# Row sums of every other head group in the last walk of an attention kernel: from strips of ones on TensorE to adds on GpSimd

## The chip, the cores and the metric

The program runs on one core of one Trainium2 chip. The metric is device time in microseconds, from the start of the execution to its end; the time of a kernel is the median of its runs. All numbers are float32 (some matmul operands are the rounded float32 form of TensorE, with the remainder in a second operand).

## The reference

Three residual layers follow one another: cross attention of 128 rows of x on 2048 rows of context, a retention layer with a gated unit, and a layer of eight experts. The change lies in the first one. Cut to what matters:

```python
x = x + xattn(layernorm(x), ctx)          # x: 8 x 128 x 512, ctx: 8 x 2048 x 512

def xattn(query_states, key_value_states):
    q, k, v = ...                         # 16 heads of 32
    scores = einsum('bhtd,bhsd->bhts', q, k) + bias
    weights = softmax(scores, axis=-1)    # over the 2048 context rows
    attn = einsum('bhts,bhsd->bhtd', weights, v)
    return attn @ wo
```

The kernel divides by the sum of the exponents after it has mixed the values: for each batch, head and row t it needs the sum over all 2048 context rows of exp(score - shift). This sum is what the change computes on another engine.

## The kernel before, in words

`attention_phase` handles 8 batches (B). The context of a batch is cut into 4 chunks (C) of 512 rows, a chunk into 4 strips (ST) of 128 rows; the 16 heads lie in 4 groups (G) of 4 heads (HG). A unit u is one head group of one chunk: u = 16 * batch + 4 * chunk + group, 128 units in all (LAST_T). Each unit is walked twice. The first walk projects keys and values and finds the row maxima (`project`, `scores`, `maxima`). The second walk comes 16 steps later (LAG) and computes the turned scores, with context rows on the partitions (`scores_turned`, L584), adds bias and maximum to them (`shift_scores`, L468 and L469 on VectorE, result in `pT`), takes the exponents in place (`exponent`, L411 on ScalarE, two operations of two heads each) and mixes the values (`mix`, L602 on TensorE, into `o_bank`).

Every engine has its own hand-written loop over steps t, and its order is that of the program. In step t TensorE issues the turned scores of unit t - 16, then the projection and scores of the first walk, then the mix of unit t - 17. From step 129 on the first walk has run out, and only turned scores and mixes remain: this is the second walk of the last batch, u = 112 to 127 (u >= LAST_U), with the output of batch 6 between the mix of unit 114 and the turned scores of unit 116.

The sums of exponents are formed in two ways. For u < 112, `add_up` on GpSimd adds the four strips of `pT` into `total[:, g]` (L365 and L369, one 128 x 512 add each; the first chunk of a batch needs three, since the first add takes two strips). `sum_up` on TensorE then sums `total` over the partitions with a matrix of ones (L643), and `invert` on VectorE takes the reciprocal from bank `misc` (L499). For u >= 112, `mix` issues 16 more matmuls of ones with `pT` right behind its own (L612, "strips"; each float32 matmul shows as two in the trace, so 32 rows a unit), which accumulate in `kv_bank`, and one reciprocal at the end takes all four groups (L528). Then `divide` (L505), `output` (L664) and `residual` (L511) close the batch.

`pT` has two buffers, chosen by u % 2. `shift_scores(u)` therefore waits until unit u - 2 has been read: by its mix (`o_mm`) and, where GpSimd adds it, by its adds (`add_step`, counted by `adds_done`). The turned scores go through 5 ring banks (`RING_PLACE`), 4 of which a unit takes; TensorE waits for a bank until VectorE has shifted out of it (`shifted`). In a batch's first chunk the shift also needs `shift0`, which a DMA brings and GpSimd completes (`first_shift`, L353), in the order of its loop: `first_shift` ahead of `add_up` in a step. Each phase is a block of its own, and the next one begins when all engines have left it.

Of the kernel before, what the change touches and what calls it, by code (L numbers as in the profile page):

```python
# [72 lines left out]
    return RING_PLACE["s", HG * a + j]  # L73


def adds_done(u):

    return ST * (u + 1) - sum(1 for w in range(u + 1) if w // G % C == 0)


def query_phase(nc, env):
# [133 lines left out]
def attention_phase(nc, env):  # L215
# [5 lines left out]
    with ExitStack() as ctx:  # L221
# [43 lines left out]
        with nc.Block() as block:  # L265
# [75 lines left out]
            @block.gpsimd  # L341
            def _(pool):
                def low_part(n, i):
                    pool.wait_ge(ctx_hi_done, n * DC + i + 1)
                    pool.tensor_tensor(ctx_lo[:, n % 2, i, :], raw[:, i % 2],  # L345
                                       ctx_hi[:, n % 2, i, :].bitcast(F32), ALU.subtract).then_inc(ctx_lo_done, 1)

                def first_shift(i):

                    pool.wait_ge(shift0_in[i % 2], 16 * (i // 2 + 1))  # L350
                    pool.wait_ge(shift_out, i + 1)
                    for s in range(2):
                        pool.tensor_tensor(shift0[:, i % 2, :, s, :], shift0[:, i % 2, :, s, :], shift[:, i % G],  # L353
                                           ALU.add).then_inc(shift0_done, 1)

                def add_up(u):

                    m, g = divmod(u, G)
                    b, c = divmod(m, C)
                    pool.wait_ge(exp_done, 2 * (u + 1))  # L360
                    parts = [pT[:, u % 2, :, i, :] for i in range(ST)]
                    if c == 0:
                        if b:
                            pool.wait_ge(total_mm, (b - 1) * G + g + 1)
                        pool.tensor_tensor(total[:, g], parts[0], parts[1], ALU.add).then_inc(add_step, 1)  # L365
                        parts = parts[2:]
                    for i, part in enumerate(parts):
                        pool.wait_ge(add_step, adds_done(u) - len(parts) + i)
                        pool.tensor_tensor(total[:, g], total[:, g], part, ALU.add).then_inc(add_step, 1)  # L369

                pool.memset(ones[:], 1.0)
                for i in range(DC):
                    low_part(0, i)
                for t in range(STEPS):
                    n, g = divmod(t, G)
                    if n < B * C - 1:
                        low_part(n + 1, g)
                    i = t - SHIFT_STEP - 1
                    if i >= 0 and i % (C * G) < G and i // (C * G) < B:
                        first_shift(i // (C * G) * G + i % (C * G))  # L380
                    u = t - LAG
                    if 0 <= u < LAST_U:
                        add_up(u)

            @block.scalar
# [61 lines left out]
            @block.vector  # L447
            def _(dve):
                def shift_scores(u):

                    m, g = divmod(u, G)
                    b, c = divmod(m, C)
                    if u < 2:
                        dve.wait_ge(turned, 2 * G)
                    else:
                        dve.wait_ge(o_mm, u - 1)
                        if u - 2 < LAST_U:
                            dve.wait_ge(add_step, adds_done(u - 2))
                    if c == 0:
                        dve.wait_ge(shift_out, b * G + g + 1)  # L460
                        dve.wait_ge(shift0_done, 2 * (b * G + g + 1))
                    for j in range(HG):
                        sc = ring[ring_st(u, j)][:].rearrange("p (i t) -> p i t", i=ST)
                        dve.wait_ge(st_mm, HG * u + j + 1)
                        i0 = 0
                        if c == 0:
                            i0 = 2
                            dve.tensor_tensor(pT[:, u % 2, j, 0:2], sc[:, 0:2], shift0[:, g % 2, j], ALU.add)  # L468
                        dve.tensor_tensor(pT[:, u % 2, j, i0:], sc[:, i0:],  # L469
                                          shift[:, g, j].unsqueeze(1).broadcast_to([P, ST - i0, T]), ALU.add  # L470
                                          ).then_inc(shifted, 1)

                def maxima(a):

                    m, g = divmod(a, G)
                    b, c = divmod(m, C)
                    for j in range(HG):
                        h = HG * g + j
                        sc = ring[ring_s(a, j)]
                        dve.wait_ge(s_mm, HG * a + j + 1)  # L480
                        if c == 0:
                            i = b * G + g
                            if j == 0:
                                dve.wait_ge(bias_in[i % 2], 16 * (i // 2 + 1))
                            dve.tensor_tensor(sc[:, 0:BW], sc[:, 0:BW], bias[:, i % 2, j, :], ALU.add
                                              ).then_inc(biased, 1)
                            dve.wait_ge(biased, HG * i + j + 1)
                        dve.tensor_reduce(negm[:, c, h:h + 1], sc[:], AX.X, ALU.max, negate=True).then_inc(max_done, 1)  # L488
                    if c == C - 1:
                        hs = slice(HG * g, HG * g + HG)  # L490
                        dve.wait_ge(max_done, HG * (a + 1))
                        dve.tensor_reduce(mneg[:, hs], negm[:, :, hs].rearrange("p c h -> p h c"), AX.X, ALU.min
                                          ).then_inc(row_max, 1)

                def invert(i):
                    dve.wait_ge(total_mm, i + 1)
                    if i % G == 0 and i >= G:
                        dve.wait_ge(wo_mm, i // G)
                    dve.reciprocal(aT[:, i % G, :], misc[:, i % G * T:(i % G + 1) * T]).then_inc(rinv_done, 1)  # L499

                def divide(b):

                    dve.wait_ge(o_mm, (b + 1) * C * G)
                    dve.wait_ge(rinv_done, (b + 1) * G)
                    dve.tensor_tensor(aT[:], o_bank[:].rearrange("p (g t) -> p g t", g=G), aT[:], ALU.mult  # L505
                                      ).then_inc(o_done, 1)

                def residual(b):
                    dve.wait_ge(wo_mm, b + 1)
                    dve.wait_ge(x_in, 16 * (b + 1))  # L510
                    dve.tensor_tensor(x_row[:], misc[:], x_row[:], ALU.add).then_inc(x_done, 1)  # L511

                for t in range(STEPS):
                    if 0 <= t - LAG < LAST_T:
                        shift_scores(t - LAG)
                    if 1 <= t <= LAST_T:
                        maxima(t - 1)
                    i = t - TOTAL_STEP
                    if i >= 0 and i % (C * G) < G and i // (C * G) < B - 1:
                        invert(i // (C * G) * G + i % (C * G))  # L520
                        if i % (C * G) == G - 1:
                            divide(i // (C * G))
                    i = t - WO_STEP - 1
                    if i >= 0 and i % (C * G) == 0 and i // (C * G) < B - 1:
                        residual(i // (C * G))
                dve.wait_ge(o_mm, B * C * G)
                dve.wait_ge(wo_mm, B - 1)
                dve.reciprocal(aT[:], kv_bank[:].rearrange("p (g t) -> p g t", g=G)).then_inc(rinv_done, G)  # L528
                divide(B - 1)
                residual(B - 1)  # L530

            @block.tensor
            def _(pe):
# [56 lines left out]
                def mix(u):  # L590
# [8 lines left out]
                    for i in range(ST):  # L599
                        for j in range(HG):  # L600
# [2 lines left out]
                                           v[:, m % (C + 1), i, h * DH:(h + 1) * DH], pT[:, u % 2, j, i, :],  # L603
                                           start=(c == 0 and g == 0 and i == 0),
                                           stop=(c == C - 1 and g == G - 1 and i == ST - 1))
                    if u >= LAST_U:

                        if u == LAST_U:
                            pe.wait_ge(kv_out, 2 * LAST_T)
                        for i in range(ST):  # L610
                            for j in range(HG):
                                mm = pe.matmul(kv_bank[j * DH:(j + 1) * DH, g * T:(g + 1) * T], ones[:],  # L612
                                               pT[:, u % 2, j, i, :], start=(c == 0 and g == 0 and i == 0),
                                               stop=(c == C - 1 and g == G - 1 and i == ST - 1))
                    mm.then_inc(o_mm, 1)

# [50 lines left out]
                for t in range(STEPS):  # L667
# [18 lines left out]
                    i = t - WO_STEP  # L686
                    if i >= 0 and i % (C * G) == 0 and i // (C * G) < B - 1:
                        output(i // (C * G))
                output(B - 1)


# [1103 lines left out]
```

## Time and profile before

| | us |
|---|---|
| runs | 2053.71, 2054.47, 2055.05 |
| median | 2054.47 |
| profiled execution | 2055.39 |
| its span, first to last instruction | 2053.6 |
| TensorE busy in the span | 1886.2 (92%) |
| VectorE | 1130.7 (55%) |
| GpSimd | 804.0 (39%) |
| ScalarE | 777.9 (38%) |

The span leaves out 1.8 us before the first and after the last instruction of the profiled execution. A busy share is an average over phases with different limits. The second walk of the last batch lies between about 1243 us, where VectorE begins to shift unit 112, and 1307 us, where the last mix is done; the retention layer starts at about 1321 us. In the views below, PE is TensorE's matmuls, PEld its weight loads, DVE VectorE, ACT ScalarE and POOL GpSimd. A line of a timeline gives start and duration, in us, of several like instructions in a row (x4: four of them), and in brackets the idle time ahead of the first and what ended it.

### The profile page before, as it was taken

Reading aid. Unit: us, or ns where it says so; the run is one execution under the profiler, and the core shown is the slowest. Engines: PE = TensorE matmul, PEld = TensorE weight load, DVE = VectorE, ACT = ScalarE, POOL = GpSimd, SP = SyncE. Lnnn points to the kernel's source line nnn. Section 1 sums busy time; section 2 is a strip of 40 time slices with the busy share of each in tenths; the row PEclk is TensorE's granted clock in tenths of the full one; section 3 lists DMA queues with packets and bytes.
Section 4 is the critical chain, followed back from the end, with each engine's and each line's share of the span. In section 5 each row is a group of like instructions: output and inputs, shape, how many; then the busy total and the mean of one; then the engine's idle time right before and its main releaser. Section 6 shows DMA issues by size and latency. Waiting matters only on the chain. (4 is left out here: it accounts for less than half of the span.)

```text
span 2053.6 us, 40698 instructions
## 1 busy us (share of the span) xinstructions
PE 1886.2 (92%) x17102; PEld 1431.3 (70%) x17102; DVE 1130.7 (55%) x2160; ACT 777.9 (38%) x1295; POOL 804.0 (39%) x641
## 2 busy tenths in 40 slices
PE   7599999999999999999999999579879998599995
PEld 3477777677677677677677777367657877499995
DVE  4244656656656556657556557464765233455553
ACT  1233434344344434344344334241244130355552
POOL 0114677668668677667667662000000000100001
PEclk9899999999999999999999999789989997699998
DMA  8622121121121122122122101210041004799993
GB/s 166 209 88 87 53 73 56 54 79 58 48 78 58 52 73 63 47 76 70 38 78 68 35 30 33 90 52 14 1 139 31 1 1 173 281 368 358 359 359 110
DMA packets 101126, 210.82 MB, mean 103 GB/s; under 512 B 9088, under 2 KB 33968, under 8 KB 95840
## 3 DMA queue, kind: packets, MB, share of 16 engines
q1 hardware_dynamic: 99488, 204.02, 29.4%
q0 software_dynamic: 1472, 4.40, 0.7%
q8 instruction: 127, 2.08, 0.4%
q14 instruction: 39, 0.32, 0.1%
HBM read 187.68 MB, written 20.71 MB: 101 GB/s over the span
## 5 line engine op out<-in xcount | busy, mean ns | idle before, releaser
L369 POOL TENSOR_TENSOR total<-total,probT 128x512 f32<-128x512 f32 x392 | 502.7, 1282 | 231.6 <-ACT probT L411 207.5
L488 DVE TENSOR_REDUCE negm<-bank 128x1 f32<-128x512 f32 x512 | 326.8, 685 | 179.4 <-PE bank L572 175.0
L469 DVE TENSOR_TENSOR probT<-bank,shift 128x512 f32<-128x512 f32 (+1 forms) x512 | 291.2, 615 | 216.2 <-PE bank L584 216.2
L411 ACT ACTIVATE probT<-probT 128x1024 f32<-128x1024 f32 x256 | 271.2, 1060 | 227.4 <-DVE probT L469 214.6
L405 ACT ACTIVATE v<-bank 128x512 f32<-128x512 f32 x128 | 76.4, 597 | 478.3 <-PE bank L552 478.3
L345 POOL TENSOR_TENSOR ctx_lo<-ctx_raw,ctx_hi 128x512 fp32r<-128x512 f32 x128 | 165.7, 1295 | 153.2 <-ACT ctx_hi L391 148.9
L552 PE MATMUL bank<-ctx_hi,wkv_hi 128*128 128x512 f32 x512 | 152.1, 419 | 22.5 <-ACT ctx_hi L391 22.5
L602 PEld LDWEIGHTS bank<-probT,v 128*32 128x32 f32 x4096 | 104.0, 109 | 94.0 <-ACT probT L411 92.0
L584 PEld LDWEIGHTS bank<-q,k 32*128 32x128 f32 x4096 | 126.0, 186 | 46.5 <-issue 44.1
L1348 POOL MEMSET zero_sb<- 128x512 f32 x1 | 0.5, 525 | 393.2 <-POOLq L1118 393.2
L552 PE MATMUL bank<-wkv_hi,ctx_hi 128*128 128x512 f32 x512 | 152.6, 420 | 0.0
L584 PE MATMUL bank<-q,k 32*128 32x128 f32 x4096 | 150.2, 283 | 0.6 <-DVE probT L469 0.5
L572 PE MATMUL bank<-k,q 32*128 32x512 f32 x1024 | 147.7, 640 | 0.0
L1670 PEld LDWEIGHTS bank<-xslotT,w_sb 128*128 128x128 f32 x1280 | 146.0, 194 | 1.9 <-DVE xslotT L1617 1.2
L1670 PE MATMUL bank<-xslotT,w_sb 128*128 128x128 f32 x1280 | 146.3, 277 | 0.8 <-DVE xslotT L1617 0.8
L602 PE MATMUL bank<-probT,v 128*32 128x128 f32 x4096 | 138.4, 276 | 6.0 <-ACT probT L411 5.8
L552 PE MATMUL bank<-wkv_lo,ctx_hi 128*128 128x512 f32 x512 | 138.0, 391 | 0.0
L552 PE MATMUL bank<-ctx_hi,wkv_lo 128*128 128x512 f32 x512 | 137.8, 391 | 0.0
L552 PE MATMUL bank<-wkv_hi,ctx_lo 128*128 128x512 f32 x512 | 136.9, 389 | 0.0
L552 PE MATMUL bank<-ctx_lo,wkv_hi 128*128 128x512 f32 x512 | 136.8, 389 | 0.0
L1593 ACT ACTIVATE w_hi<-w_sb 128x512 fp32r<-128x512 f32 x160 | 87.1, 615 | 124.8 <-PE bank L1683 79.3
L552 PEld LDWEIGHTS bank<-ctx_hi,wkv_hi 128*128 128x128 f32 x512 | 87.8, 189 | 49.7 <-ACT ctx_hi L391 23.4
(236 smaller groups left out, 2800.8 us busy)
## 6 DMA issues: line engine op xcount, KB each, us to landing
w_sb<-w SPq DMA_DIRECT2D x10, 4096.0 KB, 14.2
w_sb<-w SPq DMA_DIRECT2D x40, 1024.0 KB, 6.3
ctx_raw<-ctxT SPq DMA_DIRECT2D x128, 256.0 KB, 3.2
bias<-bias_scratch SPq DMA_DIRECT2D x32, 512.0 KB, 5.3
shift<-turned_bias SPq DMA_DIRECT2D x32, 512.0 KB, 5.1
slots<-zero_sb SPq DMA_DIRECT2D x17, 256.0 KB, 3.0
bias_scratch<-btab SPq DMA_DIRECT2D x1, 3072.0 KB, 34.2
down_w<-down SPq DMA_DIRECT2D x11, 256.0 KB, 2.6
```

The costliest lines, as they stand in the source:

```text
L345: pool.tensor_tensor(ctx_lo[:, n % 2, i, :], raw[:, i % 2], ctx_hi[:, n % 2, i, :].bitcast(F32), ALU.subtract).then_inc(ctx_lo_done, 1)
L369: pool.tensor_tensor(total[:, g], total[:, g], part, ALU.add).then_inc(add_step, 1)
L405: act.activation(v[:, n % (C + 1), g, :], (o_bank if t < LAG else kv_bank)[:], ACT.Copy).then_inc(kv_out, 1)
L411: act.activation(pT[:, u % 2, j:j + 2], pT[:, u % 2, j:j + 2], ACT.Exp).then_inc(exp_done, 1)
L469: dve.tensor_tensor(pT[:, u % 2, j, i0:], sc[:, i0:], shift[:, g, j].unsqueeze(1).broadcast_to([P, ST - i0, T]), ALU.add).then_inc(shifted, 1)
L488: dve.tensor_reduce(negm[:, c, h:h + 1], sc[:], AX.X, ALU.max, negate=True).then_inc(max_done, 1)
L552: mm = pe.matmul(dst[:], lhs, rhs, start=(c == 0 and i == 0), stop=(c == DC - 1 and i == 2))
L572: pe.matmul(ring[ring_s(a, j)][:], q[rows, b % 3, g, :], k[rows, m % C, g, :], start=True, stop=True).then_inc(s_mm, 1)
L584: mm = pe.matmul(ring[ring_st(u, j)][:, i * T:(i + 1) * T], k[rows, m % C, g, i * P:(i + 1) * P], q[rows, b % 3, g, :], start=True, stop=True)
L602: mm = pe.matmul(o_bank[j * DH:(j + 1) * DH, g * T:(g + 1) * T], v[:, m % (C + 1), i, h * DH:(h + 1) * DH], pT[:, u % 2, j, i, :], start=( ...
L1593: cp = act.activation(w2_hi[:, j, :], w2[:, j, :], ACT.Copy)
L1670: mm = pe.matmul(bank[1 + j // 4][:, j % 4 * P:(j % 4 + 1) * P], w1[:, s, c, j * P:(j + 1) * P], xT[:, c, :], start=(c == 0), stop=(c == D ...
```

## The change

In the last batch, units with an even u (groups 0 and 2) are summed by `add_up` on GpSimd as in the other batches; units with an odd u keep their strips of ones. `shift_scores(u)` waits for `add_step` wherever GpSimd adds unit u - 2. At the end TensorE sums `total` of groups 0 and 2 over the partitions into `misc`, and VectorE takes four reciprocals of 128 columns, two from `misc` and two from `kv_bank`.

```diff
--- before.py
+++ after.py
@@ -73,9 +73,14 @@
     return RING_PLACE["s", HG * a + j]
 
 
+def added_on_pool(u):
+
+    return u < LAST_U or u % 2 == 0
+
+
 def adds_done(u):
 
-    return ST * (u + 1) - sum(1 for w in range(u + 1) if w // G % C == 0)
+    return sum(ST - 1 if w // G % C == 0 else ST for w in range(u + 1) if added_on_pool(w))
 
 
 def query_phase(nc, env):
@@ -379,7 +384,7 @@
                     if i >= 0 and i % (C * G) < G and i // (C * G) < B:
                         first_shift(i // (C * G) * G + i % (C * G))
                     u = t - LAG
-                    if 0 <= u < LAST_U:
+                    if 0 <= u < LAST_T and added_on_pool(u):
                         add_up(u)
 
             @block.scalar
@@ -454,7 +459,7 @@
                         dve.wait_ge(turned, 2 * G)
                     else:
                         dve.wait_ge(o_mm, u - 1)
-                        if u - 2 < LAST_U:
+                        if added_on_pool(u - 2):
                             dve.wait_ge(add_step, adds_done(u - 2))
                     if c == 0:
                         dve.wait_ge(shift_out, b * G + g + 1)
@@ -524,8 +529,11 @@
                     if i >= 0 and i % (C * G) == 0 and i // (C * G) < B - 1:
                         residual(i // (C * G))
                 dve.wait_ge(o_mm, B * C * G)
+                dve.wait_ge(total_mm, (B - 1) * G + 1)
                 dve.wait_ge(wo_mm, B - 1)
-                dve.reciprocal(aT[:], kv_bank[:].rearrange("p (g t) -> p g t", g=G)).then_inc(rinv_done, G)
+                for g in range(G):
+                    rc = dve.reciprocal(aT[:, g, :], (kv_bank if g % 2 else misc)[:, g * T:(g + 1) * T])
+                rc.then_inc(rinv_done, G)
                 divide(B - 1)
                 residual(B - 1)
 
@@ -603,14 +611,14 @@
                                            v[:, m % (C + 1), i, h * DH:(h + 1) * DH], pT[:, u % 2, j, i, :],
                                            start=(c == 0 and g == 0 and i == 0),
                                            stop=(c == C - 1 and g == G - 1 and i == ST - 1))
-                    if u >= LAST_U:
-
-                        if u == LAST_U:
+                    if not added_on_pool(u):
+
+                        if u == LAST_U + 1:
                             pe.wait_ge(kv_out, 2 * LAST_T)
                         for i in range(ST):
                             for j in range(HG):
                                 mm = pe.matmul(kv_bank[j * DH:(j + 1) * DH, g * T:(g + 1) * T], ones[:],
-                                               pT[:, u % 2, j, i, :], start=(c == 0 and g == 0 and i == 0),
+                                               pT[:, u % 2, j, i, :], start=(c == 0 and g == 1 and i == 0),
                                                stop=(c == C - 1 and g == G - 1 and i == ST - 1))
                     mm.then_inc(o_mm, 1)
 
@@ -686,6 +694,13 @@
                     i = t - WO_STEP
                     if i >= 0 and i % (C * G) == 0 and i // (C * G) < B - 1:
                         output(i // (C * G))
+                pe.wait_ge(shift_out, B * G)
+                for g in range(0, G, 2):
+                    pe.wait_ge(add_step, adds_done(LAST_T - G + g))
+                    for j in range(HG):
+                        mm = pe.matmul(misc[j * DH:(j + 1) * DH, g * T:(g + 1) * T], ones[:], total[:, g, j, :],
+                                       start=True, stop=True)
+                mm.then_inc(total_mm, 1)
                 output(B - 1)
 
 
```

## Rows read from the trace of the kernel before

**Rows 1.** Page, part 2: GpSimd's busy tenths in 40 slices of 51.3 us

```profile
POOL 0114677668668677667667662000000000100001
```

**Rows 2.** Timeline, all engines (start us, us, engine, line, operation, out<-in), units 117 to 119

```profile
1267.08 2.48 DVE L469 TENSOR_TENSOR probT<-bank,shift 128x512 f32<-128x512 f32 x4 [0.18 <-PE bank L584]
...
1268.41 2.25 ACT L411 ACTIVATE probT<-probT 128x1024 f32<-128x1024 f32 x2 [1.01 <-DVE probT L469]
...
1270.59 2.48 DVE L469 TENSOR_TENSOR probT<-bank,shift 128x512 f32<-128x512 f32 x4 [1.02 <-PE bank L584]
...
1270.71 1.08 PE L602 MATMUL bank<-probT,v 128*32 128x128 f32 x32 [0.21 <-ACT probT L411]
...
1271.61 1.06 PE L612 MATMUL bank<-probT,att_ones 128*32 128x128 f32 x32
...
1272.62 1.17 PE L584 MATMUL bank<-q,k 32*128 32x128 f32 x32
1273.86 2.48 DVE L469 TENSOR_TENSOR probT<-bank,shift 128x512 f32<-128x512 f32 x4 [0.78 <-PE bank L584]
```

**Rows 3.** Timeline of VectorE alone: shifts of units 116, 126 and 127, the last reciprocal

```profile
1263.82 2.48 DVE L469 TENSOR_TENSOR probT<-bank,shift 128x512 f32<-128x512 f32 x4 [2.58 <-PE bank L584]
...
1298.03 2.48 DVE L469 TENSOR_TENSOR probT<-bank,shift 128x512 f32<-128x512 f32 x4 [1.02 <-PE bank L584]
1301.29 2.48 DVE L469 TENSOR_TENSOR probT<-bank,shift 128x512 f32<-128x512 f32 x4 [0.78 <-PE bank L584]
1307.00 3.36 DVE L528 RECIPROCAL aT<-bank 128x512 f32<-128x512 f32 x1 [3.22 <-issue]
```

**Rows 4.** Windows: length, busy us (count) of PE, PEld, DVE, ACT, POOL; PEclk; DMA

```profile
1263.82:1298.03 34.21, 30.64 (x960) 26.67 (x952) 25.43 (x42) 21.08 (x20) 0.00 (x0) 1.00 0.06 19
```

**Rows 5.** GpSimd: timeline, and line L369's durations (min/median/max ns)

```profile
1123.74 1.28 POOL L365 TENSOR_TENSOR total<-probT 128x512 f32<-128x512 f32 x1 [2.60 <-ACT probT L411]
1125.09 2.66 POOL L369 TENSOR_TENSOR total<-total,probT 128x512 f32<-128x512 f32 x2
...
1248.79 2.51 POOL L353 TENSOR_TENSOR shift<-shift 128x512 f32<-128x512 f32 x2 [4.29 <-DMA shift<-turned_bias]
1255.80 2.50 POOL L353 TENSOR_TENSOR shift<-shift 128x512 f32<-128x512 f32 x2 [4.50 <-DMA shift<-turned_bias]
...
L369 POOL TENSOR_TENSOR total<-total,probT x392: 1263/1286/1297, 193.9 to 1240.8; 128x512 f32<-128x512 f32 x196
```

**Rows 6.** Timeline, all engines, 1234 to 1259 us: units 110 to 115, output of batch 6

```profile
1234.36 2.25 ACT L411 ACTIVATE probT<-probT 128x1024 f32<-128x1024 f32 x2 [1.91 <-DVE probT L469]
...
1236.69 5.37 POOL L369 TENSOR_TENSOR total<-total,probT 128x512 f32<-128x512 f32 x4 [1.89 <-ACT probT L411]
...
1245.54 1.06 ACT L411 ACTIVATE probT<-probT 128x1024 f32<-128x1024 f32 x1 [0.27 <-DVE probT L469]
...
1247.22 0.43 PE L643 MATMUL bank<-total,att_ones 128*32 128x128 f32 x8 [0.20 <-ACT shift L426]
...
1248.03 0.95 DVE L499 RECIPROCAL aT<-bank 128x128 f32<-128x128 f32 x1
...
1253.16 0.42 DVE L468 TENSOR_TENSOR probT<-bank,shift 128x256 f32<-128x256 f32 x1 [0.74 <-PE bank L584]
...
1257.94 1.06 PE L612 MATMUL bank<-probT,att_ones 128*32 128x128 f32 x32
1258.50 0.42 DVE L468 TENSOR_TENSOR probT<-bank,shift 128x256 f32<-128x256 f32 x1 [2.60 <-POOL shift L353]
...
1258.93 3.27 PE L664 MATMUL bank<-wo_sb,aT 128*128 128x512 f32 x7
```

**Rows 7.** Timeline of TensorE's matmuls in later phases, at the lower clock

```profile
1430.29 2.09 PE L1041 MATMUL bank<-qT,kT 32*128 32x128 f32 x32
...
1508.69 1.97 PE L1242 MATMUL bank<-ident,z 128*128 128x128 f32 x8 [2.89 <-DVE z L1186]
```

**Rows 8.** Window of TensorE: length, busy us (matmuls), mean granted clock, DMA share, GB/s

```profile
1507.00:1508.00 1.00, 0.00 (x0) 0.89 0.00 0
```

## Prediction

> **What bounds the kernel now.** The page's slices come first: GpSimd's digits are zero in the slices behind 1283 us [rows 1], although TensorE still works at attention there. So the engine that the change uses is free in that stage; what has to be found is what paces the stage. The chain of waits doesn't reach back this far, so I read the timeline of all engines over the last sixteen units, u = 112 to 127.
>
> One unit goes through the engines in this order: VectorE shifts its scores (four L469 operations), ScalarE takes exponents (two L411), TensorE mixes (L602), then the strips of ones (L612), then the turned scores of a later unit (L584). Follow unit 117 in [rows 2]: the shift starts at 1267.08; ScalarE runs from 1268.41 to 1270.66, 3.58 behind that start; the mix starts at 1270.71, the strips at 1271.61, the turned scores of unit 119 at 1272.62, and its shift at 1273.86. That loop is 6.78 us for two units. A second loop ties neighbours together: the five ring banks let the turned scores of a unit start only when three of the four shift operations of the unit before have read theirs. From the shift of 118 at 1270.59 to the turned scores of 119 at 1272.62 it is 2.03, and 1.24 more to the shift at 1273.86, so 3.27 for one unit. Two of those are 6.54, less than 6.78. **The pace of the stage is therefore the two-unit loop, strips included.** From the shift of 116 to that of 126 it is 34.21 us [rows 3], five pairs of 6.77 with one excess of 0.36.
>
> There are two interleaved copies of the two-unit loop: even units follow even units, odd units follow odd ones, and neither can run ahead of the other by more than the ring lets it. TensorE is busy 30.64 of these 34.21 us at the full granted clock [rows 4], but its mix waits for ScalarE in every unit, so it is not the work on TensorE alone that sets the pace.
>
> **The change, part by part.** *Removed:* the strips of the eight even units, 32 matmuls each, 1.06 us a group [rows 2]. This shortens only the even copy of the loop. The odd copy keeps its strips and its 6.78, and an even unit can't be followed by the next odd one any faster than that copy allows. In units 116 to 126 the removal alone is worth nothing. It is worth something in one place: between unit 114 and unit 116 the output matmuls of the batch before stand behind the strips of 114 on TensorE. The strips start at 1257.94 and the output at 1258.93, and the shift of 116 at 1263.82 waits for what follows that output [rows 3, 6]: 0.99 earlier.
>
> *Added on GpSimd:* the sums of eight units: three adds each for 112 and 114 (the first chunk begins with the sum of two parts), four each for 116 to 126. They start 0.08 behind the exponents: ScalarE ends at 1236.61, GpSimd starts at 1236.69, and the four take 5.37 [rows 6]. Three take 4.01, from 1123.74 to 1127.75 [rows 5]. The 392 adds of this line lie between 1263 and 1297 ns, beside any mix of VectorE and ScalarE work [rows 5], so I take the same durations here.
>
> *Added on VectorE:* the wait at the head of each shift. The kernel holds the exponents in two buffers by parity, so unit u overwrites what unit u-2 left. Before, this stage waited only for the mix of u-2; now an even unit also waits for GpSimd's sum of u-2. Queued behind that wait are this unit's shift, then the next odd unit's, and with them all exponents, mixes and turned scores: nothing in the stage runs past it.
>
> Price of the new loop, even unit to even unit: 3.58 from the shift to the end of the exponents [rows 2], 0.08 to GpSimd, 5.37 for four adds [rows 6], and the handover from GpSimd to VectorE. The only row that shows one is L353, which ends at 1258.30, and the shift behind it at 1258.50 [rows 5, 6]: 0.20. Together **9.23 us for two units, where 6.78 stood**. The odd unit between them follows at 3.27 and is hidden. From 116 to 126 this is five times 9.23, 46.15 in place of 34.21: **+11.94**. The handover lies between the 0.08 of ScalarE to GpSimd and, as an upper bound, twice the row, 0.40; over five turns that is -0.6 to +1.0. I take 0.20, the same pair of engines.
>
> *Ahead of 116:* GpSimd's queue also holds L353, which prepares the shifts of 114 and 115, behind the new adds. Exponents of 112 end at 1246.60 [rows 6]; its adds then run from 1246.68 to 1250.69, and the L353 that ran at 1248.79 [rows 5] moves to about 1250.77, ends at 1253.28, and lets the shift of 114 start at 1253.48 in place of 1253.16 [rows 6]: 0.32 late. The mix of 114 is late by as much, so of the 0.99 above 0.67 stays. The next L353 starts at 1255.80, when its transfer lands [rows 5]; it is not late, and neither is unit 115. The adds of 114 stand behind it, 1258.38 to 1262.39; with the handover 1262.59, ahead of the 1263.15 at which 116 can start. That cover is 0.56 wide; without it the -0.67 shrinks, no more. **Sum of this part: -0.67.**
>
> *The end:* before, the reciprocal starts 8.97 behind the shift of 126 [rows 3]. Now the adds of 126 end 3.58 + 0.08 + 5.37 = 9.03 behind it; TensorE then sums over the partitions of group 2, eight matmuls in 0.43 [rows 6], with handovers on both sides. No row shows GpSimd to TensorE, so I take the 0.20 again (0.08 to 0.40), and 0.12 to VectorE from L612, which ended at d+5.59 in [rows 2], against the reciprocal 5.71 behind the shift of 127 [rows 3]. That is 9.78: +0.81. The four reciprocals of 128 columns take at least the 3.36 of the one of 512 [rows 3] and at most four times 0.95 [rows 6], +0 to +0.44; I take +0.2. Everything behind attention starts when this block ends and moves with it.
>
> **Sum: -0.67 + 11.94 + 0.81 + 0.2 = +12.3 us.** The profiled execution took 2055.39 (its span 2053.6 and 1.8 around it); it becomes 2067.7. It lies 0.9 above the median of the runs, 2054.47, from which I forecast **2066.8**. With the handovers, the adds at their shortest and longest, and the starts of later stages against the clock (about a microsecond either way) the forecast's own range is 2064 to 2070.
>
> **The rivals.** *TensorE's work is the bound, and the adds stay ahead: faster.* For it: TensorE is busy nine tenths of the stage [rows 4]. Then each removed group would give its 1.06: eight are -8.5, less 0.6 for sums and reciprocals at the end, 2046.6. It decides only if a pair can be done in 6.78 - 1.06 = 5.72, so four adds in 5.72 - 3.58 - 0.28 = 1.86. They take 5.37. Chance 0.03.
>
> *The adds hide, but the odd units hold the pace: no change.* It needs four adds within 6.78 - 3.86 = 2.92, or a wait that isn't reached because something else in a pair takes longer. Then -0.99 at the output and about +0.6 at the end: 2054.1. Against it stands the same 5.37. Chance 0.04.
>
> *The clock falls as well: slower still.* With the new loop TensorE idles in each pair from the end of the odd unit's strips (3.27 + 5.59 = 8.86 behind the even shift) to the next turned scores (9.23 + 2.03 = 11.26), 2.4 us. Elsewhere a gap of 2.89 ended at 1508.69, and the granted clock had fallen below 1.00 in the microsecond from 1507 [rows 7, 8]; in this stage before, it never fell [rows 4]. At the lower level of 1.2 GHz a group of turned scores takes 2.09 [rows 7] in place of 1.17 [rows 2]. Two such groups cost 1.84 a pair, and the even unit's scores are ready 9.23 - 6.54 = 2.69 ahead of GpSimd: one fall is hidden. Only if TensorE stays low for whole pairs does it decide: its five groups (1.17 + 1.17 + 1.08 + 1.08 + 1.06 = 5.56) would take up to 11.1, so 0 to 1.9 more a pair, and one or two at the end. Six more is the middle: 2072.8. Chance 0.08.
> The Trainium skill, "TensorE: Matmul & The Clock Gate", section "A second HAM failure mode: psum-queue depth-cycling", speaks for this rival: short, frequent idles between groups of matmuls made the clock swing between its levels in another kernel. By that rule the sum would be the 2072.8 of this rival. The trace of this stage, with idles of 0.2 us in each unit and a clock of 1.00 [rows 2, 4], doesn't show it.
>
> **How the numbers follow.** The forecast has 0.85, the clock 0.08, no change 0.04, faster 0.03. The range goes from 2062.5, where handovers and adds are all short and something still overlaps, to 2072.5, most of the way to the clock's case. About 4.1 us, 0.2%, is what a measurement of this kernel can tell from no change: faster 0.03, same 0.04, slower 0.93.
>
> **What would show it.** In the changed profile the shifts of even units from 118 on wait for GpSimd (L369), not for turned scores, 9.2 apart; the odd ones follow at 3.3; GpSimd shows back-to-back fours of 5.4 with 3.8 between them. The strips are left in odd units only. The reciprocals start near 1319. I am wrong if the even shifts still wait for TensorE, or if the pairs stand at 6.8. A pair well above 9.3 with matmuls of double length would be the clock.

## The result, and the profile after

The changed kernel takes 2065.01 us (median of five runs, 2063.61 to 2066.58) against 2054.47 before: 10.5 us more, a ratio of 1.0053 with a 95% interval of 1.0038 to 1.0068. The forecast was 2066.8. The profiled execution took 2065.77, with a span of 2063.9 (10.3 more than before).

In the page's slices GpSimd is now busy to the end of the stage (before: [rows 1]):

```profile
POOL 0114678668677667677677766300000000100001
```

The timeline of all engines, one pair of units (118 and 119) and the shift of 120, to be held against [rows 2]:

```profile
1272.02 2.48 DVE L474 TENSOR_TENSOR probT<-bank,shift 128x512 f32<-128x512 f32 x4 [3.34 <-POOL total L374]
1273.34 2.25 ACT L416 ACTIVATE probT<-probT 128x1024 f32<-128x1024 f32 x2 [3.57 <-DVE probT L474]
...
1275.29 2.48 DVE L474 TENSOR_TENSOR probT<-bank,shift 128x512 f32<-128x512 f32 x4 [0.78 <-PE bank L592]
...
1275.67 5.34 POOL L374 TENSOR_TENSOR total<-total,probT 128x512 f32<-128x512 f32 x4 [3.74 <-ACT probT L416]
...
1278.91 1.08 PE L610 MATMUL bank<-probT,v 128*32 128x128 f32 x32 [0.42 <-ACT probT L416]
...
1279.81 1.06 PE L620 MATMUL bank<-probT,att_ones 128*32 128x128 f32 x32
1281.10 2.49 DVE L474 TENSOR_TENSOR probT<-bank,shift 128x512 f32<-128x512 f32 x4 [3.33 <-POOL total L374]
```

The shift of 118 starts at 1272.02, its exponents end at 1275.59, GpSimd adds from 1275.67 to 1281.01, and the shift of 120 starts at 1281.10: 9.08 us for two units, where [rows 2] had 6.78. VectorE sat idle for 3.33 us ahead of it, and the profile names GpSimd's add as what ended the wait. The odd unit between them follows its neighbour by 3.27, as in [rows 2]. The strips (now L620) stand behind the odd unit only.

VectorE's waits from 1262 to 1320 us (who waited for whom: us in total, times, longest):

```profile
DVE probT L474 <- POOL total L374: 12.9, 4, 3.3
DVE probT L474 <- PE bank L592: 6.5, 7, 1.5
DVE probT L474 <- PE bank L620: 3.7, 1, 3.7
```

Four of the five even shifts are put down to GpSimd. The fifth, unit 124, is put down to the strips of 123. These are its rows: GpSimd's adds of 122, the strips of 123, the shift of 124:

```profile
1293.84 5.35 POOL L374 TENSOR_TENSOR total<-total,probT 128x512 f32<-128x512 f32 x4 [3.74 <-ACT probT L416]
...
1298.42 1.06 PE L620 MATMUL bank<-probT,att_ones 128*32 128x128 f32 x32
1299.63 2.49 DVE L474 TENSOR_TENSOR probT<-bank,shift 128x512 f32<-128x512 f32 x4 [3.69 <-PE bank L620]
```

The name is misleading. The program lets the shift of 124 wait for the mix and the adds of 122, not for the strips of 123; they only ended last, at 1299.48, 0.29 behind the adds. In the run below that keeps all strips, the shift of 124 starts at 1299.20, before the strips of 123 end at 1299.45, and is put down to GpSimd. So all five even shifts follow GpSimd. The shift of 124 starts 0.44 behind the adds, where the others start 0.09 behind them; these 0.35 are found at unit 124 in every kernel (last section). Stage 116 to 126 as a window, to be held against [rows 4] (length; busy us and instructions of PE, PEld, DVE, ACT, POOL; granted clock; DMA share; GB/s):

```profile
1262.93:1308.72 45.79, 31.64 (x864) 26.67 (x864) 25.44 (x41) 21.14 (x20) 25.55 (x20) 0.93 0.05 14
```

The same ten units take 45.79 us in place of 34.21. TensorE lists 864 matmuls in place of 960 (without five groups of strips, but with the mix and the strips of unit 125, which before fell behind the window) and yet 31.64 us busy in place of 30.64: the clock was at its lower level for part of the time. VectorE and ScalarE do the same work as before.

The end of the stage, unit 126 to the division (against [rows 3]):

```profile
1312.37 5.33 POOL L374 TENSOR_TENSOR total<-total,probT 128x512 f32<-128x512 f32 x4 [3.74 <-ACT probT L416]
...
1317.26 1.06 PE L620 MATMUL bank<-probT,att_ones 128*32 128x128 f32 x32
...
1318.14 0.62 PE L701 MATMUL bank<-total,att_ones 128*32 128x128 f32 x16
...
1318.88 3.39 DVE L535 RECIPROCAL aT<-bank 128x128 f32<-128x128 f32 x4 [3.66 <-PE bank L620]
1322.38 0.69 DVE L510 TENSOR_TENSOR aT<-bank,aT 128x512 f32<-128x512 f32 x1
```

Stretch by stretch the two profiled executions differ like this (each from the start times named, the first number of each row after, the second before):

| stretch | after | before | difference |
|---|---|---|---|
| first instruction to the shift of 112 | 1242.55 | 1242.76 | -0.21 |
| shift of 112 to shift of 116 | 20.38 | 21.06 | -0.68 |
| shift of 116 to shift of 126 | 45.79 | 34.21 | +11.58 |
| shift of 126 to the reciprocal | 10.16 | 8.97 | +1.19 |
| reciprocal to division | 3.50 | 3.46 | +0.04 |
| division to the store of the last rows | 7.60 | 7.88 | -0.28 |
| that store to the last instruction | 733.92 | 735.24 | -1.32 |

### The profile page after: what moved, and what is told of

Read it like the earlier page. It is cut to its first block and busy times, and to the rows that moved or that the text cites. A ratio compares the mean times of both kernels' runs of the same rounds, so it can differ in the third digit from the quotient of the medians.

```text
span 2063.9 us, 40260 instructions
## 1 busy us (share of the span) xinstructions
PE 1883.1 (91%) x16862; PEld 1427.5 (69%) x16862; DVE 1131.2 (55%) x2163; ACT 778.4 (38%) x1295; POOL 843.5 (41%) x671
## 5 line engine op out<-in xcount | busy, mean ns | idle before, releaser
L374 POOL TENSOR_TENSOR total<-total,probT 128x512 f32<-128x512 f32 x420 | 539.3, 1284 | 256.1 <-ACT probT L416 230.3
## 6 DMA issues: line engine op xcount, KB each, us to landing
bias_scratch<-btab SPq DMA_DIRECT2D x1, 3072.0 KB, 34.2
```

## The experiments

The theory: the pace is now the loop through one exponent buffer, from the shift of an even unit over ScalarE and four GpSimd adds to the shift two units later. The rivals: TensorE's emptier stage and its clock; GpSimd working beside VectorE; and, for what the removed strips are worth, TensorE's work as the bound. Stretches of stage are those from the shift of 116 to that of 126. The kernel before ran beside them: 2054.44 in the first four, 2053.63 in the last two. The ratios are formed over all runs and need not be the quotient of the two medians.

**A third buffer for the even units.** This takes away what the wait is for, and nothing else.

```diff
+        spare = v[:, (B - 1) * C % (C + 1) - 1].rearrange("p i d -> p (i d)").rearrange(
+            "p (j i t) -> p j i t", j=HG, i=ST)
+
+        def buffer(u):
+            return spare if u >= LAST_U and u % 4 == 2 else pT[:, u % 2]
...
-                        if added_on_pool(u - 2):
-                            dve.wait_ge(add_step, adds_done(u - 2))
+                        before = u - 4 if u >= LAST_U + 2 and u % 2 == 0 else u - 2
+                        if added_on_pool(before) and u != LAST_U + 2:
+                            dve.wait_ge(add_step, adds_done(before))
```

> The changed kernel with one more exponent buffer for the even units 114, 118, 122 and 126 (in the space of a chunk of values that is no longer read), so that an even unit waits for the adds of four units before, not of two. Nothing else is changed: the adds, the removed strips and the sums at the end stay. Theory of the buffer loop (exponents, four adds, the wait of the shift two units later): GpSimd needs 5.4 us a pair, less than 6.77, so no shift waits for it any more; the odd units hold the pace, units 116 to 126 take 34.2 us again in place of 45.8, and the time is 2054.5 (0.9 gained at the output of batch 6, about as much lost at the end), give or take 1. If TensorE's work were the bound without that wait, the removed strips would show and it would be near 2047. If the cost came from the clock of an emptier TensorE or from GpSimd working beside VectorE, it would stay near 2065, for both are still there.

Measured: 2053.92 us, 1.0002 of the kernel before (0.9993 to 1.0011). The stage took 33.78. VectorE's and GpSimd's timelines, two lines of each:

```profile
1269.40 2.48 DVE L480 TENSOR_TENSOR v<-bank,shift 128x512 f32<-128x512 f32 x4 [0.81 <-PE bank L598]
...
1276.18 2.48 DVE L480 TENSOR_TENSOR probT<-bank,shift 128x512 f32<-128x512 f32 x4 [0.81 <-PE bank L598]
```

```profile
1273.06 5.36 POOL L379 TENSOR_TENSOR total<-total,v 128x512 f32<-128x512 f32 x4 [1.20 <-ACT v L421]
1279.83 5.37 POOL L379 TENSOR_TENSOR total<-total,probT 128x512 f32<-128x512 f32 x4 [1.42 <-ACT probT L421]
```

GpSimd does the same adds, in the same 5.36, VectorE's shifts take the same 2.48 beside them, and no shift waits for the adds: pairs are back at 6.78. So it is the wait on the buffer that cost the time, not GpSimd's work beside VectorE. It also answers the other question: with the wait gone and the eight groups of strips still removed, the kernel is not faster than before. The odd units, with their strips, hold the pace. One turn of theirs, from the shift of 125 over its exponents, mix and strips and the turned scores of 127 to the shift of 127:

```profile
1293.34 2.48 DVE L480 TENSOR_TENSOR probT<-bank,shift 128x512 f32<-128x512 f32 x4 [0.78 <-PE bank L598]
...
1294.66 2.25 ACT L421 ACTIVATE probT<-probT 128x1024 f32<-128x1024 f32 x2 [1.01 <-DVE probT L480]
...
1296.96 1.08 PE L616 MATMUL bank<-probT,v 128*32 128x128 f32 x32 [0.42 <-ACT probT L421]
...
1297.86 1.06 PE L626 MATMUL bank<-probT,att_ones 128*32 128x128 f32 x32
...
1298.85 1.17 PE L598 MATMUL bank<-q,k 32*128 32x128 f32 x32
1300.11 2.48 DVE L480 TENSOR_TENSOR probT<-bank,shift 128x512 f32<-128x512 f32 x4 [1.00 <-PE bank L598]
```

It closes after 6.77 us without a gap. A little of the removal does show, 33.78 against 34.21: two of the five pairs stand at 6.55, twice the 3.27 that the ring allows between neighbours. The profiled execution, at 2056.72 the second slowest of its eleven, loses more than that at the end: 11.06 us from the shift of 126 to the reciprocal, in place of 8.97, with the clock at its lower level over the last strips (0.50 from 1305 to 1307 us). TensorE's work as the bound (2047) is out.

**The strips of the even units left in as well.** Only the removal is undone.

```diff
-                    if not added_on_pool(u):
+                    if u >= LAST_U:
...
-                        if u == LAST_U + 1:
+                        if u == LAST_U:
```

> The changed kernel with the strips of ones of the even units left on TensorE as well (their results in the bank are not used; the sums come from GpSimd). Only the removal is undone; adds and wait stay. Theory of the buffer loop: the pairs stay at 9.09 us, 116 to 126 at 45.5 to 45.8, the output of batch 6 is 0.9 later again; time 2065.9, from which about 0.3 may go if the fuller TensorE keeps its clock at the end. Theory that an emptier TensorE (its clock) makes it slow: near 2054.5.

Measured: 2064.7 us, 1.0054 (1.0038 to 1.0069). The shifts of 118 and 120:

```profile
1271.62 2.48 DVE L474 TENSOR_TENSOR probT<-bank,shift 128x512 f32<-128x512 f32 x4 [3.34 <-POOL total L374]
...
1280.69 2.48 DVE L474 TENSOR_TENSOR probT<-bank,shift 128x512 f32<-128x512 f32 x4 [3.33 <-POOL total L374]
```

9.07 a pair, 45.76 for the stage: with TensorE as full as before the change, the stage is as long as with it emptier. An emptier TensorE is not the cause. This run alone doesn't settle the clock, since it falls here too. But the falls lie in other pairs than in the changed kernel. TensorE in the same four microseconds, within the pair from 118 to 120, first in this run, then in the changed kernel (length, busy us and matmuls, granted clock, DMA share, GB/s):

```profile
1274.00:1278.00 4.00, 3.58 (x83) 0.62 0.00 0
```

```profile
1274.00:1278.00 4.00, 2.94 (x88) 1.00 0.00 0
```

The pair with the fall takes 9.07 us, the pair without it 9.08. The pace of the stage is not the clock's. The strips of 114 are back ahead of the output, and from the shift of 112 to that of 116 it is 21.27 us in place of the change's 20.38, the 0.89 that was expected. The median lies 0.3 below that of the change; 0.6 to 0.9 above it was expected. The end is 0.57 shorter (below), and what is left of the miss lies within the spread of the four and five runs (1.8 and 3.0 us).

**Three adds and one strip in each even unit; two and two.** The length of GpSimd's part of the loop is changed, and the sums stay whole (`parts_on_pool` is 3 or 2 for the even units; the partial sums go into the bank of the strips).

```diff
-                    parts = [pT[:, u % 2, :, i, :] for i in range(ST)]
+                    parts = [pT[:, u % 2, :, i, :] for i in range(parts_on_pool(u))]
...
-                        for i in range(ST):
+                        for i in range(parts_on_pool(u), ST):
...
-                        mm = pe.matmul(misc[j * DH:(j + 1) * DH, g * T:(g + 1) * T], ones[:], total[:, g, j, :],
-                                       start=True, stop=True)
+                        mm = pe.matmul(kv_bank[j * DH:(j + 1) * DH, g * T:(g + 1) * T], ones[:], total[:, g, j, :],
+                                       start=False, stop=(g == G - 2))
```

Three:

> In the even units of the last walk GpSimd adds three of the four strips and TensorE takes the fourth as a strip of ones; at the end the partial sums are added into the same bank and one reciprocal is taken. Theory of the buffer loop: a pair is 3.57 + 0.08 + 4.01 + 0.09 = 7.75 us, still over the 6.77 of the odd units; 116 to 126 take 38.8 to 39.1, 4.6 over before; about 0.5 gained at the output, 0.6 lost at the end: 2059. A clock or a TensorE cause: nearly as slow as the change, 2064 to 2065, since only a quarter of the strips is back.

Two:

> As the one before, with two strips added on GpSimd and two on TensorE in the even units. Theory of the buffer loop: 3.57 + 0.08 + 2.65 + 0.09 = 6.39 us, under the 6.77 at which the odd units go, so the wait no longer decides: 116 to 126 in 34.2 to 34.6, time 2054.5 to 2055. If the adds cost by their number, without such a point, half of the cost would stay: 2060.

Measured: three adds 2059.74 us, 1.0025 (1.0013 to 1.0036), stage 39.01; two adds 2054.28, 1.0002 (0.9992 to 1.0011), stage 33.78. First two shifts and GpSimd's part with three adds, then VectorE's waits with three and with two adds (1262 to 1306 us):

```profile
1272.25 2.48 DVE L479 TENSOR_TENSOR probT<-bank,shift 128x512 f32<-128x512 f32 x4 [1.98 <-POOL total L379]
...
1279.97 2.48 DVE L479 TENSOR_TENSOR probT<-bank,shift 128x512 f32<-128x512 f32 x4 [1.98 <-POOL total L379]
```

```profile
1275.90 3.99 POOL L379 TENSOR_TENSOR total<-total,probT 128x512 f32<-128x512 f32 x3 [3.74 <-ACT probT L421]
```

```profile
DVE probT L479 <- POOL total L379: 10.3, 5, 2.3
DVE probT L479 <- PE bank L597: 5.3, 6, 2.0
```

```profile
DVE probT L479 <- PE bank L597: 11.6, 12, 2.3
```

One add less takes 1.36 off a pair, 9.08 to 7.72, which is the add. The next one would take it to 6.4, but it stops at 6.77, where the odd units go (two of the five pairs at 6.56, as with the third buffer, hence 33.78 and not the 34.2 expected), and the wait for GpSimd is gone from the list. The cost isn't one per add: it has the point that the prediction put between two adds and three (2.92 us for all of them; two take 2.64, three 3.99).

**Both loops taken apart.** If the two loops pace the stage, a kernel in which both are loosened must be faster than either. From unit 114 on there are four exponent buffers, from 116 on a mix is issued behind the turned scores of the second unit after it, and from 118 on a sixth ring bank is used. GpSimd sums the even units up to 122.

```diff
-                    if 0 <= t - LAG - 1 < LAST_T:
+                    if 0 <= t - LAG - 1 < LATE_U:
                         mix(t - LAG - 1)
+                    if LATE_U <= t - LAG - 2 < LAST_T - 1:
+                        mix(t - LAG - 2)
...
+        if t - LAG == WIDE_U:
+            free.insert(0, RING_BANKS)
...
+        def buffer(u):
+            return spare[u % 2] if u >= LAST_U and u % 4 >= 2 else pT[:, u % 2]
...
-    return u < LAST_U or u % 2 == 0
+    return u < LAST_U or (u % 2 == 0 and u < LAST_T - G)
```

> A version that takes both loops apart: from unit 114 on four exponent buffers (two more, in the space of values and bias that are no longer read), from unit 116 on the mix of a unit behind the turned scores of the second unit after it, from unit 118 on a sixth ring bank; the even units 112 to 122 are summed on GpSimd as in the change, 124 and 126 by strips, and the partial sums go into the same bank ahead of the last mix. If the pace is set by the two loops as described, none of them holds it any more: it falls to GpSimd's 5.4 us a pair or to the engines' own work, 2.7 to 2.9 us a unit from 118 on in place of 3.39 before, and the time is 2048.5, give or take 1.5. If GpSimd working beside VectorE, or TensorE's clock, were what slowed the change, it would be no faster than 2054.5.

The same with all strips on TensorE and no adds in the last walk:

> The same three changes with all strips of the last walk left on TensorE and nothing on GpSimd: what the buffers, the later mix and the bank are worth without the change. TensorE's own work, 1.10 + 0.79 + 1.09 = 3.0 us a unit, should then be the pace from 118 on; nine units at 0.39 less than before: 2051, give or take 1. If it is as fast as the version with GpSimd, the adds on GpSimd are worth nothing even where they are hidden.

Measured: with GpSimd 2047.84 us, 0.9973 (0.9963 to 0.9983); without it 2049.85, 0.9981 (0.9972 to 0.9990). Both are faster than the kernel before, and so than the changed one. The second lies just under the 2050 to 2052 expected; the kernel before was 0.8 faster beside these runs than the 2054.47 from which it was reckoned. Shifts and adds with GpSimd, 1270 to 1284 us:

```profile
1273.04 2.48 DVE L485 TENSOR_TENSOR probT<-bank,shift 128x512 f32<-128x512 f32 x4 [0.56 <-PE bank L603]
...
1276.69 5.35 POOL L384 TENSOR_TENSOR total<-total,probT 128x512 f32<-128x512 f32 x4 [0.35 <-ACT probT L426]
...
1278.76 2.48 DVE L485 TENSOR_TENSOR v<-bank,shift 128x512 f32<-128x512 f32 x4 [0.56 <-PE bank L603]
...
1282.41 5.35 POOL L384 TENSOR_TENSOR total<-total,v 128x512 f32<-128x512 f32 x4 [0.36 <-ACT v L426]
```

A pair takes 5.72 us and the stage 29.17, against 34.21 before; GpSimd, idle 0.36 between its fours, is close to its own limit there, and nobody waits for it. Without GpSimd the stage takes 29.92, a unit 2.99, which is TensorE's work. So most of the gain belongs to the buffers, the later mix and the bank together; what each of the three is worth was not tried. What the adds on GpSimd themselves add is 0.75 us in this stage and 0.70 ahead of it (20.36 and 21.06 from the shift of 112 to that of 116, since the strips of 114 are gone ahead of the output), less 0.10 at the end: 1.35 in the profiles. In the medians it is 2.0; the two intervals against the kernel before overlap, and the nine runs and the eleven, set against each other, differ by 1.6 in the mean (95% interval about 0.2 to 3.0). So the adds are likely to help a little, and the times show no more.

## Why the prediction was right, point by point

*The pace of the stage before.* Two interleaved copies of a two-unit loop, each with its strips: the third buffer leaves the strips of the even units out, hides the adds, and still three of five pairs stand at 6.77 or more and two at 6.55; the turn of the odd units shown there closes at 6.77. This step held.

*Ahead of 116.* Forecast -0.67, measured -0.68, and that is luck in part: two terms were mis-sized and cancel. TensorE's matmuls before, from the mix of 114 over the output to the turned scores of 116, and the same three in the changed kernel:

```profile
1257.04 1.08 PE L602 MATMUL bank<-probT,v 128*32 128x128 f32 x32 [0.43 <-ACT probT L411]
...
1258.93 3.70 PE L664 MATMUL bank<-wo_sb,aT 128*128 128x512 f32 x8
1262.56 1.17 PE L584 MATMUL bank<-q,k 32*128 32x128 f32 x32
```

```profile
1257.00 1.08 PE L610 MATMUL bank<-probT,v 128*32 128x128 f32 x32 [0.48 <-ACT probT L416]
1258.01 3.70 PE L672 MATMUL bank<-wo_sb,aT 128*128 128x512 f32 x8
1261.64 1.17 PE L592 MATMUL bank<-q,k 32*128 32x128 f32 x32
```

From the mix to the output it is 1.01 us in place of 1.89: without the strips 0.88 is gained, not 0.99. And the shift of 114, counted from that of 112, is 0.16 late (10.56 in place of 10.40), not 0.32. The transfer for unit 115 landed later, so that GpSimd began its `first_shift` at 1256.33 in place of the 1255.80 of [rows 5], and 115 started 0.5 later. That didn't reach unit 116: its turned scores start 3.63 behind the output in both kernels, and 3.63 behind it also in the run with the strips kept, where that transfer landed early (1254.20).

*The new loop.* Forecast 9.23 a pair, measured 9.08 to 9.09. The exponents (3.57), the start of GpSimd (0.08) and the adds (5.34) are within 0.03 of what was read from the rows of before. The term that was mis-sized is the handover from GpSimd to VectorE: 0.20 from the one row that showed it, [rows 5, 6], and 0.09 here (1281.01 to 1281.10). Five turns make 0.55 of it, a little more with the adds at 5.34. The other way goes the 0.35 of unit 124, which is in the 34.21 of before and which I had left out of my five pairs. So the loop added 11.58 us in place of 11.94.

*The end.* Forecast +0.81 to the reciprocal, measured +1.19. The run with the strips kept had 9.59 from the shift of 126 to the reciprocal, the change 10.16: in the change the clock fell behind 1310.75 and unit 127 started 4.02 behind 126 in place of 3.27, so that its strips ended at 1318.32, later than the adds (1317.70); with the strips kept it didn't fall there. This is the clock's rival, at the one place where nothing hid it, and it cost 0.57. Without it the term would have been +0.62: with the strips kept it is 0.61 from the end of the adds to the reciprocal, where 0.75 was forecast. The four reciprocals cost 0.03 more than the one of 512 columns, not 0.2.

*What hides the clock.* The prediction said that one fall a pair stays hidden behind GpSimd. TensorE's matmuls and the granted clock in the changed kernel:

```profile
1283.14 1.69 PE L592 MATMUL bank<-q,k 32*128 32x128 f32 x32 [2.27 <-DVE probT L474]
1284.76 1.94 PE L610 MATMUL bank<-probT,v 128*32 128x128 f32 x32
```

```profile
1283.00:1284.00 1.00, 0.86 (x24) 0.81 0.00 0
1284.00:1285.00 1.00, 1.00 (x24) 0.50 0.00 0
1285.00:1286.00 1.00, 1.00 (x24) 0.50 0.07 16
```

The clock went to its lower level of 1.2 GHz after 2.27 us of idleness, the shift of 121 came 3.75 behind that of 120 in place of 3.27, and the shift of 122 still started 9.09 behind that of 120, with a wait for GpSimd shortened from 3.33 to 2.86. It stayed hidden, as forecast; the rival of a clock that decides for whole pairs did not come about.
The Trainium skill, "TensorE: Matmul & The Clock Gate", section "A second HAM failure mode: psum-queue depth-cycling", says of another kernel that frequent short idles between groups of matmuls made the clock swing between its two levels, at a loss of throughput. The trace agrees for the changed stage in that the clock swings there (mean 0.93, where [rows 4] had 1.00), but ahead of the falls stand idles of 1.8 to 2.3 us, and the idles of 0.2 to 0.4 in each unit before the change left it at 1.00. What the falls cost here is 0.57 us, since GpSimd's loop covers the rest.

*Behind attention.* I let everything move with the end of the block. It did, but for -0.28 in the output matmuls and -1.32 behind them. In the profiles of this study this rest lies between 733.9 and 735.5, without order by how late it starts, which is about the microsecond either way that I had allowed. What fixes it in a single run was not tried.

The four terms of the sum came to +12.1 where +12.3 was forecast, the loop 0.4 under and the end 0.2 over its forecast; the rest of the miss, 1.8, lies in stretches for which I had nothing: -0.21 ahead of the stage and -1.60 behind the division. The range (2062.5 to 2072.5) and the forecast's own (2064 to 2070) hold the 2065.0.

## What to carry to other kernels

Before work is moved to an idle engine, look at what that engine will hold while it works. Here it held one of two buffers for 5.4 us in a stage that needs the buffer back after 6.8, behind 3.6 of other work: the engine had time, the buffer had not. And count the copies of a loop: taking work out of every other turn shortens nothing while the turns in between keep it; of the two remedies, the buffers (with the later mix and the sixth bank) gave most, and the idle engine's help was worth little behind them.

## What the runs showed of the hardware that I had not expected

- The clock fell behind idle stretches of only 2.3 us (at 1283 and 1311 us above), and a third time at about 1294, behind idles of 1.79 and 0.42. It didn't fall behind every such stretch: 2.28 us ahead of 1274.05 in the changed kernel were followed by no fall, 2.3 us at the same place in the kernel with the strips kept were (0.62 as mean of 1274 to 1278 us). In this stage before the change, with idles of 0.2 to 0.4 in each unit, it never fell.
- The handover from GpSimd's add to the shift took 0.09 us. That from GpSimd's `first_shift` to the shift of unit 115 took 0.20 in the changed kernel too (1258.82 to 1259.02), as in [rows 5, 6]: it depends on the pair of instructions, not on the engines alone. Why was not tried.
- In every kernel of this study the shift of unit 124 comes 0.35 us later than its neighbours' pattern (before: 7.13 in place of 6.77; three adds: 8.08 in place of 7.73), whatever the pace. It belongs to a place in the program and not to a time, and the delay is VectorE's: it starts 0.44 to 0.47 behind its last releaser there, whether that is TensorE (before) or GpSimd (three adds), where its neighbours start 0.06 to 0.09 behind theirs. In all eight profiles one packet of 8 KB on an instruction queue (q14) starts 0.66 to 0.68 us behind that shift, and none other on it within 40 us. So a fetch of VectorE's program is a candidate; that it is the cause is not shown.
